# Sparse-coding kernel: each set's small solve moved out of the other set's scan

## What is computed

```python
G = D.T @ D + 1e-5 * eye(256)            # D: 512 x 256, columns of norm 1
h_bar = (D.T @ X).T ; h = h_bar          # one row of 256 per patch
for k in 1..5:
    index = argmax(abs(h) where not yet picked)
    # row k of the Cholesky factor of G[I, I]: a triangular solve over the picks
    # x_stack: the coefficients of the picks so far, two triangular solves
    h = h_bar - x_stack @ G[I]
recon = D @ coeffs                       # added to x
```

## Time and profile before

| quantity | value |
|---|---|
| runs (3) | 554.5, 556.13, 557.31 us; median 556.13 us |
| the profiled execution | 555.17 us, of which its span 553.3 us |
| mean granted clock of PE | 0.891 of full speed |
| busy in the span | PE 409.0, DVE 458.7, ACT 309.3, POOL 149.8 us |

### The profile page before, as it was taken

The page is one execution under the profiler, slowest core; times in us unless marked ns, Lnnn a source line. Parts: engine busy times, 40 slices in busy tenths (PEclk is TensorE's granted clock), DMA queues, the critical chain, the costliest instruction groups (busy, mean ns, idle before and its releaser), DMA issues.

```text
span 553.3 us, 7423 instructions
## 1 busy us (share of the span) xinstructions
PE 409.0 (74%) x1666; PEld 296.3 (54%) x1666; DVE 458.7 (83%) x2325; ACT 309.3 (56%) x682; POOL 149.8 (27%) x162
## 2 busy tenths in 40 slices
PE   0099885899666669889893979998839557788674
PEld 0032772355556556456682854567738435676453
DVE  4483657878898979969999899989998999799990
ACT  2544436586656467668687385976802443465133
POOL 3000035334200063522300464433003644330010
PEclk9999996989878688989997979999978866899598
DMA  5979212789400025997510277613101754124155
GB/s 101 173 104 170 60 39 68 126 131 156 91 0 2 0 81 115 201 175 115 127 26 1 63 168 150 134 57 78 39 0 30 176 130 100 52 67 96 39 113 115
DMA packets 110202, 50.71 MB, mean 92 GB/s; under 512 B 103632, under 2 KB 104144, under 8 KB 110160
## 3 DMA queue, kind: packets, MB, share of 16 engines
q1 hardware_dynamic: 102000, 26.13, 28.9%
q0 software_dynamic: 8160, 24.13, 18.9%
HBM read 34.24 MB, written 8.65 MB: 78 GB/s over the span
## 4 chain that ended last, share of the span: by engine, by line
PE 43%; DVE 31%; ACT 8%; issue 6%; SPq 6%; DMA 5%; DVEq 0%; ACTq 0%
PE h L387 30%; PE conv_ps L387 10%; DVE junk L992 8%; DVE coef L1113 4%; DVE top L922 3%; DMA xb<-in_x 3%; SPq L248 3%; DVE top_i L935 3%; DVE top_i L937 2%; ACT score L636 2%; PE back_ps L387 2%; ACT diag L645 2%; ACT xb L602 2%; SPq L255 2%; DVE coef L1109 1%
## 5 line engine op out<-in xcount | busy, mean ns | idle before, releaser
L359 POOL DMA_INDIRECT rows<-gram,idx_u x128 | 131.5, 1027 | 346.7 <-DVEq L979 317.2
L387 PE MATMUL h<-rows,diag 128*128 128x256 f32 x640 | 165.9, 420 | 49.8 <-ACT diag L645 47.6
L387 PEld LDWEIGHTS h<-rows,diag 128*128 128x128 f32 x640 | 133.0, 212 | 83.6 <-issue 60.0
L645 ACT ACTIVATE diag<-ident,dx 128x128 f32<-128x128 f32 x320 | 96.8, 387 | 40.6 <-DVEq L1094 37.5
L992 DVE SCALAR_TENSOR_TENSOR junk<-mask,rows 128x256 bf16<-128x256 bf16 x320 | 119.4, 421 | 0.0
L636 ACT ACTIVATE score<-h 128x512 f32<-128x512 f32 x80 | 47.3, 597 | 99.4 <-PE h L387 99.0
L922 DVE MAX8 top<-score 128x8 f32<-128x256 f32 x160 | 65.3, 422 | 33.9 <-ACT score L636 32.3
L387 PE MATMUL h<-d_sb,z 128*128 128x256 f32 x256 | 66.6, 424 | 3.5 <-DVEq L913 2.5
L387 PE MATMUL back_ps<-coef_t,d_t 128*128 128x256 f32 x224 | 58.3, 419 | 13.3 <-ACT coef_t L651 13.3
L387 PEld LDWEIGHTS h<-d_sb,z 128*128 128x128 f32 x256 | 63.2, 330 | 6.9 <-issue 3.2
L387 PE MATMUL conv_ps<-xa,w_taps 128*64 128x512 f32 x128 | 61.7, 604 | 1.4 <-ACT x L614 1.0
(11 more groups left out here) (152 smaller groups left out, 506.0 us busy)
## 6 DMA issues: line engine op xcount, KB each, us to landing
xa<-in_x SPq DMA_DIRECT2D x64, 128.0 KB, 5.4
out<-x SPq DMA_DIRECT2D x64, 128.0 KB, 2.9
x<-y POOLq DMA_DIRECT2D x14, 512.0 KB, 4.7
xb<-in_x SPq DMA_DIRECT2D x42, 128.0 KB, 4.2
rows<-gram,idx_u POOLq DMA_INDIRECT x128, 3.1
xb<-in_x SPq DMA_DIRECT2D x14, 120.0 KB, 5.2
rows<-in_x SPq DMA_DIRECT2D x6, 128.0 KB, 4.4
d_sb<-in_L_conv_dictionary SPq DMA_DIRECT2D x4, 128.0 KB, 4.0
```

The source lines that it names most:

```text
L359: pool.indirect_dma_start(out=rows[s][:, k, t, :], out_offset=None, in_=gram_dram[:, :], in_offset=bass.IndirectOffsetOnAxis(ap=idx_u[s][: ...
L387: return nc.tensor.matmul(dst, lhs, rhs, start=start, stop=stop, skip_group_check=skip)
L645: last = nc.scalar.activation(diag[s][:, t, j, :], ident[:, :], ACT.Copy, scale=dx[s][:, k, t, j:j + 1])
```

## The change

Two scans on DVE no longer carry the other set's solve. It is run to its end just ahead of them.

```diff
                         beside[0] = norm_params(f, 1, y_root, y_params)
+                    run(chain[1])
                     if k:
-                        scan(r, 0, k, together(chain[1], beside[0]), 1)
+                        scan(r, 0, k, beside[0], 1)
                     else:
                         scan(r, 0, k)
                     select(r, 0, k, rows_of)
                     chain[0] = solve(r, 0, k)
                     extract(r, 0, k, chain[0])
-                    scan(r, 1, k, together(chain[0], beside[1]), 0)
+                    run(chain[0])
+                    scan(r, 1, k, beside[1], 0)
```

## The result

The changed kernel takes 565.31 us (median of four runs, 563.46 to 565.95), the kernel before 555.94 us (four runs, 554.5 to 557.31). The ratio is 1.0163, with 95% from 1.0127 to 1.0199: the kernel is slower by 9.4 us. The profiled execution took 564.86 us with a span of 563.0 us, 9.7 us more than before, at the same mean granted clock of 0.891. The forecast was 565.6 us, and +9.5 us for the profiled execution.

The account below looks back on a forecast made before the run. DVE and PE were taken to set the end in turns, in a ring with ACT. Added DVE time less filled waits gave -1.1, +2.0, +4.9 and +3.7 us by round, +9.5 us: 565.6 us for the median, range 554.5 to 576 us.

Parts of the forecast that it names:

- The price of a bare solve: On DVE, 0.20 us per dependent operation; nine cost 1.03 us more than threaded in steps 1 and 2, about 1.1 in step 3.
- Step 4's rest: The six operations left of set 0's step-4 solve: about 1.55 us bare, 0.9 us more than threaded.
- step 0's: The three operations of a step-0 solve: 0.6 us bare against 0.2 threaded, 0.4 us more.
- The waits it fills: DVE's added 32 us partly fills its 32.3 us of waits for scores, which fall below 20 us.
- By round: Change at the ends of rounds 0 to 3: -1.1, +2.0, +4.9 and +3.7 us, together +9.5 us.
- The mechanism of round 0: Diagonals of set 1, step 3 start 3.9 us earlier, removing scan(1,4)'s 1.64 us wait; the round ends 1.1 us earlier.
- What the profile would show: Solve blocks of 1.8 to 2.0 us, scans of 3.4 us, DVE's score waits and ACT's line-1094 waits each below 20 us.
- One sign of being wrong: The forecast is wrong if the convolution stretches get longer or shorter by more than 1 us.
- its 1 to 2 us: The marker that h was read comes 1 to 2 us later; PE's correlation waits for it, but its scores are wanted later.
- Rival 1: The waits swallow all of DVE's added 32 us as the ring tightens everywhere: 553 to 559 us, chance 0.18.
- Rival 2: A bare operation on DVE costs no more than a threaded one, 0.10 us; only savings remain: 546.6 us, chance 0.11.
- Rival 3: No waits are filled, because DVE's lateness reaches POOL's gathers and PE's updates: up to 32 us, 588 us, chance 0.09.

Follow-up runs that it names:

- run 1: The changed kernel with set 1's solves threaded again, so only set 0's run bare: 559.62 us, ratio 1.0053.
- run 2: The changed kernel with set 0's solves threaded again, so only set 1's run bare: 557.66 us, ratio 1.0016.
- run 3: The changed kernel with solves still bare, but the diagonals released only inside the next scan, at its tenth call: 564.69 us, ratio 1.0127.
- run 5: The kernel before with only the solves of steps 0 to 2 bare: 561.07 us, ratio 1.0069.
- run 6: The kernel before with only the solves of step 3 and the rest of set 0's step-4 solve bare: 566.04 us, ratio 1.0161.
- run 7: The kernel before with only set 1's step-2 solve bare in every round, and all of set 1's in round 0: 554.16 us, ratio 0.9957.
- run 8: The changed kernel measured again without an edit, on the chip of the by-step variants: 564.33 us, ratio 1.0133.
- run 11: Second measurement of the changed kernel with the marker that h was read given ahead of the bare solve: 567.21 us, ratio 1.0228.
- run 4: The changed kernel with the marker that h was read given ahead of the bare solve, first measurement: 569.42 us, ratio 1.0226.
- run 10: The changed kernel with one independent 128x4 operation behind each operation of a bare solve, 260 in all: 570.45 us, ratio 1.0282.
- run 9: The kernel before, all solves threaded, but in steps 1 to 3 one solve operation at each place of a scan instead of two: 566.38 us, ratio 1.0207.

## Why the prediction was right

- **The price of a bare solve** was taken from norm_params, and its pitch of 0.20 us was met in the blocks of steps 1 and 2 (in step 3 it is 0.22). The term was a little small: 1.15 to 1.26 us more than threaded in rounds 1 to 3, not 1.03 to 1.1. The block waits 0.11 us behind the last pick, near the 0.1 forecast, but also 342.63 - 342.49 = 0.14 us from the end of its last operation to the next MAX8, which the sum had left out. Step 4's rest (0.80 for 0.9) and step 0's (0.13 in d2 for 0.4) were smaller than I took, so that the sum per round came out right all the same: 8.3 us, not 8.0.
- **The waits it fills.** 25.7 us of the 32.3 in the earlier trace rows went. The forecast had 32 us added and, with +9.5 left, 22.5 given back; the runs have 33.3 and 25.7. By the count this leaves +7.6 us, against +9.7 in the span. With the waits at MAX8 that have no releaser taken in, it is within 2.3 us of the span in runs 1, 2, 3, 5, 6, 7, 8 and 11 as well, mostly below it. It fails in run 4 (+9.8 against +14.3) and run 10 (+8.8 against +15.3), where gaps inside the blocks are a part of what it misses. So added work less filled waits gives sign and size for the change and its parts, not the last 2 us, and not every variant.
- **By round** the forecast was -1.1, +2.0, +4.9, +3.7 us, measured -2.9, +1.6, +6.2, +3.3, and +1.6 in the tail where I had nothing. The mechanism of round 0 was there: the diagonals of set 1, step 3, which had waited until 156.02 us, started at 150.11 us. That is 5.9 us earlier, not 3.9. Round 2 lost 1.3 us more than I took: six solves at some 0.15 us more are 0.9 of it. The total is partly luck: round 0's larger gain hides the larger losses. Run 8, which had the clock of the kernel before in 99 to 131 us, bears this out: its round 0 has -1.2 us, near what the forecast said, and its span grew by 11.5, not 9.5.
- **What the profile would show.** Block, scan length and the waits for scores (6.6, below 20) came as said. ACT's waits for line 1094 fell to 26.0 us only, not below 20. One sign of being wrong did appear: from set 0's choice in step 1 to that in step 3 (d3 to d6) the stretch with the convolutions was 2.0 us shorter in round 0, 1.1 shorter in round 1 and 2.7 longer in round 2. The forecast's own terms had -0.8, -0.8 and some +2 there, so PE's pace did not stay quite as it was. "DVE is busy as long as before" was wrong: it was busy 21 us longer, since overlap was lost. Nor did I foresee PE's 22.1 us at the marker. I had called its 1 to 2 us harmless, and the early markers of runs 4 and 11 bear out that nothing is won by having them back.
- **Rival 1** (the waits swallow it all) failed: 25.7 us filled is less than 33.3 added, and round 2 had little to fill.
- **Rival 2** (bare costs as threaded) is refuted by the block: 0.20 us a step against 0.10. The Trainium skill, "VectorE: DVE Perf Modes", section "Rules for kernel authors", advises for chained operations to keep their number small, and not the semaphores. For small dependent operations this trace does not agree: the same nine, with the same waits, cost 0.89 us threaded and 2.05 bare. The remark in its section "The DRAIN you can't avoid" that an operation that is not held starts earlier does agree, by the 0.08 us of run 10's fillers.
- **Rival 3** (nothing is filled) failed, with 6.6 us of waits left.
- **The chances** of the forecast and the rivals add up to 0.98, those of faster, same and slower to 1.00; 0.02 has no owner.

**What the diagnosis lacked** is the other half: run 9 shows that in the kernel before less work on DVE is no gain by itself. Moving either way, to bare or to thin, costs 9 to 12 us. A kernel in which DVE's work and the ring's length are near each other would behave so; that is my explanation, and no run tests it by itself.

## What to carry to other kernels

A chain of small dependent operations on DVE costs its latency when it stands alone (0.20 us a step) and half or less when it is threaded between independent ones; whoever pulls it out to release a consumer sooner should count the added time against the waits at the next operation, stretch by stretch. Where those waits are long it is cheap (d6), where the engine is full it is lost nearly one for one. And a threaded chain shares every wait of its host: where the ring is the bound, keep it dense at the host's front: threaded thinly, with the diagonals some 1 us later, this kernel took 2% longer.

## What the runs showed of the hardware that was not expected

- The gap in a chain of dependent DVE operations can be filled: an independent 128x4 operation between each two left the chain at 0.21 us a step in the mean (run 10).
- DVE's busy time is no measure of its work: 458.7 and 479.8 us for the same 2325 instructions.
- A bare solve can have single gaps of 0.4 to 0.7 us in which DVE waits for no other engine (run 10, round 0). Their cause is open.
- The time of one kernel often goes with the clock that PE was granted. Over 19 runs of the kernel before on one chip (553.2 to 562.1 us, mean granted clock 0.889 to 0.907) the two have a correlation of -0.82, over 23 runs on another -0.73, but over 11 on a third only -0.34. The profiled executions of before and after agree in the mean, 0.891, and differ by 9.7 us, so the loss is not that alone. On another chip the changed kernel was granted less (run 8, 0.884 to 0.890) than the kernel before (0.889 to 0.907); whether that adds to its time or follows from a PE that idles more is open.
